# The mask of a windowed attention added by VectorE instead of TensorE, and the row maximum subtracted by GpSimd

## The reference, cut to what matters

```
sim  = einsum('bhwie,bhwje->bhwij', bq, bk2) * QK_SCALE        # 32 x 64 scores a window
mask = (it < jb) | (it > jb + w) | (jb == -1)
sim  = where(mask, -finfo.max, sim)
attn = softmax(sim, -1)
out  = einsum('bhwij,bhwje->bhwie', attn, bv2)
```

## Time and profile before

| | us |
|---|---|
| three timed runs | 5191.45, 5195.39, 5198.09; median 5195.39 |
| the profiled execution: span from its first to its last instruction | 5196.3 |
| its own time | no other figure than its span |
| busy: TensorE, VectorE, ScalarE, GpSimd | 4059.5, 4157.5, 2852.2, 2552.5 |
| one round inside a turn of the loop, and one that begins a turn | 87.4, 91.1 |

### The profile page before, as it was taken

How to read it: one execution, slowest core, us unless ns; L and a number is a source line. 1 busy time by engine, 2 the same in 40 slices (tenths; PEclk the granted TensorE clock), 3 DMA queues, 4 the chain that set the end, 5 groups by cost and what they waited for, 6 DMA issues and landing times. The chain is left out here.

```text
span 5196.3 us, 147973 instructions
## 1 busy us (share of the span) xinstructions
PE 4059.5 (78%) x62298; PEld 2893.8 (56%) x63066; DVE 4157.5 (80%) x6032; ACT 2852.2 (55%) x4736; POOL 2552.5 (49%) x1604
## 2 busy tenths in 40 slices
PE   2012048999979999789999789999799997899996
PEld 2011036666656666566666566666566665666664
DVE  5977978888878888778888788888788887788885
ACT  1011036666656666556666566666566665565665
POOL 3665844544435544445455445445355444454542
PEclk8566579999989999999999999999899999999998
DMA  0000011111111111111111111111111111111112
GB/s 21 0 6 6 0 43 37 25 25 25 25 45 25 25 25 25 33 37 25 25 25 25 33 37 25 25 25 25 46 25 25 25 25 33 37 25 25 25 25 57
DMA packets 86314, 139.19 MB, mean 27 GB/s; under 512 B 14457, under 2 KB 35600, under 8 KB 83984
## 3 DMA queue, kind: packets, MB, share of 16 engines
q1 hardware_dynamic: 78698, 127.06, 9.3%
q10 hardware_dynamic: 6950, 2.39, 0.2%
HBM read 30.59 MB, written 4.46 MB: 7 GB/s over the span
## 5 line engine op out<-in xcount | busy, mean ns | idle before, releaser
L1054 POOL TENSOR_TENSOR kn<-kn,r 128x512 f32<-128x512 f32 x385 | 495.6, 1287 | 1659.0 <-ACT r L968 1659.0
L960 ACT ACTIVATE sq<-ps 128x512 f32<-128x512 f32 x768 | 459.3, 598 | 905.8 <-PE ps L784 901.7
L1090 DVE TENSOR_TENSOR rb<-ps,tab 128x512 f32<-128x512 f32 x768 | 527.7, 687 | 404.7 <-PE ps L784 346.1
L966 ACT ACTIVATE r<-r 128x512 f32<-128x512 f32 x769 | 485.7, 632 | 567.3 <-DVE r L1101 566.7
L1054 POOL TENSOR_TENSOR qn<-qn,r 128x512 f32<-128x512 f32 x384 | 495.4, 1290 | 550.0 <-ACT r L968 550.0
L1047 POOL TENSOR_TENSOR kn<-ra,rb 128x512 f32<-128x512 f32 x384 | 631.2, 1644 | 79.7 <-DVE ra L1092 70.2
L1094 DVE TENSOR_TENSOR sqlo<-sq 128x512 fp32r<-128x512 f32 x768 | 644.9, 840 | 0.0
L782 PE MATMUL ps<-xhs,wl 128*128 128x512 f32 x768 | 403.5, 525 | 237.3 <-PEq L122 178.5
L1101 DVE TENSOR_SCALAR r<-ps 128x512 f32<-128x512 f32 x768 | 524.2, 683 | 29.0 <-remote 10.5
L1047 POOL TENSOR_TENSOR qn<-ra,rb 128x512 f32<-128x512 f32 x384 | 537.6, 1400 | 0.0
L857 PEld LDWEIGHTS ps<-v,pt 64*32 64x32 f32 x24768 | 394.2, 108 | 243.7 <-issue 186.9
(11 more groups left out here) (182 smaller groups left out, 9161.1 us busy)
## 6 DMA issues: line engine op xcount, KB each, us to landing
v<-v SPq DMA_DIRECT2D x96, 768.0 KB, 5.8
v<-v SPq DMA_DIRECT2D x96, 192.0 KB, 5.7
raw<-in_L_ffn_Wqkv SPq DMA_DIRECT2D x7, 1536.0 KB, 7.3
tab<-in_rotary SPq DMA_DIRECT2D x6, 1024.0 KB, 5.7
raw<-in_L_ffn_Wo SPq DMA_DIRECT2D x6, 512.0 KB
sT<-so ACTq DMA_DIRECT2D x3, 768.0 KB, 3.3
xnat<-in_L_attn_hidden_states SPq DMA_DIRECT2D x8, 256.0 KB, 3.4
srow<-sT SPq DMA_DIRECT2D x8, 256.0 KB, 3.1
```

Source lines behind the costliest of these rows:

```text
L960: nc.scalar.activation(sq[:, k, :], ps[:, A, :], ACT.Square).then_inc(cur["sq"], 1)
L966: nc.scalar.activation(r1[:, k, :], r1[:, k, :], ACT.Ln, scale=RN * RN).then_inc(cur["ln"], 1)
L1054: nc.gpsimd.tensor_tensor(dst, dst, r1[:, k, :], ALU.mult).then_inc(cur["qkn"], 1)
L1090: nc.vector.tensor_tensor(rb[:, k, :], ps[:, BB, :], tab[:, 2 * k + 1, :], ALU.mult)
```

## The change

TensorE no longer writes the mask; its scores start their banks anew. VectorE adds the mask, which stays in float32 in the constants' tile, as it moves the scores from PSUM to `pr`, and takes the maximum from `pr`. GpSimd subtracts the maximum in place, at the end of its iteration. There is a new counter "masked": TensorE's scores wait for it, where they waited for "sub", which GpSimd now counts and exp waits for as before. The bf16 copies of the mask and of the identity in the setup are gone, and a block's end waits for GpSimd's last subtraction too.

```diff
             def scores(i):
-                after(pe, "sub", before(i, 1))
-                for e in range(2):
-                    nc.tensor.matmul(ps[:, S0 + e, 0:256], identb[:], maskb[:], start=True, stop=False,
-                                     skip_group_check=True)
+                after(pe, "masked", before(i, 1))
                 pe.wait_ge(cur["qkn"], 2 * i + 1)
...
-                            k[:, wd * WIN:(wd + 2) * WIN], start=False, stop=True, skip_group_check=True,
+                            k[:, wd * WIN:(wd + 2) * WIN], start=True, stop=True, skip_group_check=True,
...
+            def subtract_max(i):                       # GpSimd
+                b = (i - 1) % 2
+                pool.wait_ge(cur["m"], i + 1)
+                p8 = pr[:, b, :].rearrange("p (g k) -> p g k", g=8)
+                nc.gpsimd.tensor_tensor(p8, p8, stat[:, b, 0, :].unsqueeze(2).broadcast_to([P, 8, 64]),
+                                        ALU.subtract).then_inc(cur["sub"], 1)
+
             for i in range(HP):
                 if live(i, 1):
                     normalise(i, 1)
...
                     normalise(i, 0)
+                if live(i, 1):
+                    subtract_max(i)
...
-            def subtract_max(i):
+            def row_max(i):                            # VectorE, called where subtract_max was
                 b = (i - 1) % 2
                 dve.wait_ge(cur["S"], i + 1)
-                s4 = ps[:, S0:S1 + 1, 0:256].rearrange("p e (g k) -> p e g k", g=4)
                 after(dve, "pt", before(i, 2))
-                nc.vector.tensor_reduce(stat[:, b, 0, :].rearrange("p (e g) -> p e g", e=2), s4, AX_X,
+                nc.vector.tensor_tensor(pr[:, b, :].rearrange("p (e k) -> p e k", e=2), ps[:, S0:S1 + 1, 0:256],
+                                        mask.unsqueeze(1).broadcast_to([P, 2, 256]),
+                                        ALU.add).then_inc(cur["masked"], 1)
+                dve.wait_ge(cur["masked"], i + 1)
+                nc.vector.tensor_reduce(stat[:, b, 0, :], pr[:, b, :].rearrange("p (g k) -> p g k", g=8), AX_X,
                                         ALU.max).then_inc(cur["m"], 1)
-                dve.wait_ge(cur["m"], i + 1)
-                nc.vector.tensor_tensor(pr[:, b, :].rearrange("p (e g k) -> p e g k", e=2, g=4), s4,
-                                        stat[:, b, 0, :].rearrange("p (e g) -> p e g", e=2).unsqueeze(3)
-                                        .broadcast_to([P, 2, 4, 64]), ALU.subtract).then_inc(cur["sub"], 1)
```

More of the change, by code:

```diff
@@ L542, in transformer @@
     tab = sb("tab", [P, 4, S])
-    maskb = sb("maskb", [P, 256], BF16)
-    identb = sb("identb", [P, P], BF16)
+    mask = con[:, C_MASK:C_MASK + 256]
     pairr = sb("pairr", [P, P], F32R)
@@ L570, in transformer @@
     s_w = sem("s_w")
-    names = ("xh v vev ab sq sl rot g ssq r ln add qkn S m sub exp rs ri pt ptev o oev ot otev wo x1 "
+    names = ("xh v vev ab sq sl rot g ssq r ln add qkn S masked m sub exp rs ri pt ptev o oev ot otev wo x1 "
              "fx mean fc fq var fe fr fn fh fl w1 gx gl h w2 x2 shifted cleared").split()
@@ L646, in _ @@
             nc.vector.memset(xT[:, B, :], 0.0).then_inc(s_hi, 1)
-            nc.vector.tensor_copy(maskb[:], con[:, C_MASK:C_MASK + 256]).then_inc(s_hi, 1)
-            nc.vector.tensor_copy(identb[:], ident).then_inc(s_hi, 1)
             nc.vector.tensor_copy(pairr[:], con[:, C_PAIR:C_PAIR + P]).then_inc(s_hi, 1)
             nc.vector.tensor_copy(pairb[:], con[:, C_PAIR:C_PAIR + P]).then_inc(s_hi, 1)
-            dve.wait_ge(s_hi, 7)
+            dve.wait_ge(s_hi, 5)
             dve.wait_ge(s_vz, 3)
@@ L759, in round_ @@
         counts = {**dict.fromkeys("rot g ssq add qkn".split(), 2 * HP),
-                  **dict.fromkeys("oev ptev otev sub o S ri ot pt".split(), HP), "xh": 4}
+                  **dict.fromkeys("oev ptev otev sub masked o S ri ot pt".split(), HP), "xh": 4}
         def after(eng, name, n):
@@ L1175, in vector @@
                 if live(i, 1):
-                    subtract_max(i)
+                    row_max(i)
                 if i == 2 and full:
@@ L1202, in _ @@
                 pool.wait_ge(sets[0]["qkn"], 1 if drain else 2 * HP)
+                pool.wait_ge(sets[0]["sub"], 1 if drain else HP)
             @block.vector
@@ L1232, in _ @@
                 pool.wait_ge(sets[0]["qkn"], 2 * HP)
+                pool.wait_ge(sets[0]["sub"], HP)
             @block.sync
```

## The result

The changed kernel takes 5462.4 us (median of 4, 5454.9 to 5466.6) against 5195.1: 1.0509 times the time before, 95% interval 1.0496 to 1.0521. Slower, as forecast, and 3 us from the forecast time.

A forecast was written before the change was run, and what follows sets the result against it. No engine is full; a loop between VectorE and TensorE sets the iteration. 255 us over 48 rounds, 16 at block ends and about 1 of drain make 272 on 5196.3; forecast 5465 us, range 5350 to 5560.

The forecast's parts named there:

- Mask matmuls and VectorE's pair at nothing: Removing TensorE's mask matmuls (119 us) gains zero; VectorE's new add and maximum cost the same as its old pair.
- The order in i=6, 2.84 us: In iteration 6 exp starts 2.84 us late, because GpSimd's subtraction stands behind the put-off normalise(5,0); nothing covers it.
- The subtraction, 1.29 us: GpSimd's new 128x512 subtraction takes 1.29 us per iteration, with 1.10 and 1.55 kept as alternatives.
- my lower bound of 1.10: Cheapest GpSimd subtraction considered, 1.10 us, a sixth of a broadcast product; about 4.5 us a round, 5426 in all.
- 2.10: Time from the old L1111's start until exp can start, via maximum, semaphores and GpSimd's subtraction: 2.10 us.
- i=4 and i=5, 0.67 and 1.15: Iterations 4 and 5 lengthen by exp's full delay, 0.67 and 1.15 us, since consumers stand right behind exp.
- i=0, 1 and 2, 0, 0.06 and 0.60: Iterations 0, 1 and 2 lengthen by 0, 0.06 and 0.60 us, existing waits covering the rest of exp's delay.
- the long wait for guard(0,0): In iteration 0, TensorE's squares(0,1) waits for VectorE's guard(0,0) longer than exp's 0.71 us delay, so cost 0.
- The clock stays up: TensorE's granted clock does not fall in iteration 6's stall; the rival that it falls had chance 0.18, 5550 us.
- my price of 1.8 us a round: Estimated cost if TensorE's clock fell in iteration 6: 1.8 us in each of 48 rounds, 85 us more.
- Ends of blocks, 16 us: At two barriers per layer GpSimd's last subtraction ends 1.35 us later than VectorE's did; times 12, 16 us.
- 5.32 us a round: Lengthening of one round of eight iterations: 0.67 + 1.15 + 2.84 + 0.06 + 0.60; 255 us over 48 rounds.

The follow-up runs named there:

- e3: The kernel before without the mask matmuls, scores left unmasked, all else as it was: 5206.7 us, 1.0014.
- e2: The changed kernel with added matmuls in iteration 6 that only keep TensorE busy while it waits for exp and normalise: 5384.8 us, 1.0359.
- e1: The changed kernel with GpSimd's subtraction in iteration 5 moved ahead of normalise(5,0): 5267.5 us, 1.0132.
- e7: The kernel before with GpSimd's rotations of i = 0, 1, 2 and 5 waiting for VectorE's split of the squares: 5072.1 us, 0.9761.
- e4: The changed kernel with the subtraction on VectorE behind the maximum, in place in SBUF, instead of on GpSimd: 5350.6 us, 1.0295.
- e5: e1 with ScalarE's v copies of iterations 2 and 4 and gates of iteration 5 ahead of exp: 5256.7 us, 1.0103.

## Why the prediction was right, and where its parts were not

- *Mask matmuls and VectorE's pair at nothing*: right, by e3 and by 1366 against 1371 ns.
- *The order in i=6, 2.84 us*: right in mechanism. e2, which has the wait and not the clock, gives 13.94 - 11.27 = 2.67; e1 without it 0.09, and that is not the subtraction's: without the mask matmuls alone (e3) i=6 is 11.37 too.
- *The subtraction, 1.29 us*: too dear. 1.04 us is its median, under my lower bound of 1.10, which came from broadcast products of another shape. Exp could start 1.84 us after the old L1111, not 2.10.
- *i=4 and i=5, 0.67 and 1.15*: 0.41 and 0.94; the difference, 0.26 and 0.21, is the cheaper subtraction.
- *i=0, 1 and 2, 0, 0.06 and 0.60*: measured -0.49, -0.36 and +0.17. Here a step failed: I had seen that a late GpSimd lets the split go ahead in i=1, and let squares(i,1) wait for a late turn_out instead; for i=0 I kept the long wait for guard(0,0). In the changed kernel the split takes 0.86 us in i=0 instead of 1.67, and squares(0,1) to squares(2,1) follow turn_out without a wait for guard. With the cheaper subtraction turn_out is earlier, so a gain remains. How much of it is the split's and how much the subtraction's, no run separates; e7 shows that in the kernel before the split's order alone is worth more, 1.00 in i=0 and 0.70 in i=1.
- *The clock stays up*: failed. It fell in 45 of 48 rounds and cost 78 us (e2); my price of 1.8 us a round was near the 1.7 measured.
- *Ends of blocks, 16 us*: ScalarE's pause before the next layer's weights, at the end of five blocks, was 4.88 to 5.45 us and is 5.99 to 6.43, 1.1 us more in the mean, as 1.35 less the 0.25 of the cheaper subtraction makes it. At the other six ends, behind lone rounds, i=7 takes 18.70 us in e1 and e2 against 17.46, 1.24 more (medians). The twelve come to some 14. (The row at 2178.06 is the end of a block of seven rounds, not of a lone round; the count is the same.)

So 5.32 us a round without the clock was too much by 2.04 (98 us over 48 rounds; e2's round is 3.28 us above that before), and 78 us of clock and some 30 at ends of blocks, turns of the loop and the first rounds of a layer, half of which I had counted, filled the place. The time was hit by luck, because two errors cancelled; the direction and the place were right for the reason given, that exp(6) could not start earlier in the order that the code gives.

## What to carry to other kernels

An idle engine is not a free one: in an in-order program ask what the moved instruction queues behind, at each place of the loop, above all where another step was put off; here that one place made 195 of 267 us, with the clock that fell in its stall. Moved ahead of one instruction, the same subtraction on the same engine beat the version on VectorE (e1 and e4). Look also for gaps that an edit opens on TensorE: in e5 the clock's fall took back most of what the edit had won. When a change makes an engine late and some iterations get shorter, look for what it got out of the way of: that contention was worth 2.4% by one wait, in the unchanged kernel.

## What the runs showed of the hardware

- A GpSimd subtraction with one operand broadcast along rows of 64 took 1.04 us, the same shape with two full operands 1.29. Size didn't tell it, nor did the products of the earlier trace rows. The 1.29 is a product's, and a sum of two full operands took 1.28 where nothing held it; no subtraction of two full operands was run, so that it is the broadcast which makes it cheaper is not shown.
- TensorE's clock fell to its lower level (0.50) after two gaps of 1.41 and 1.80 us with about 1 us of work between them, in 45 of 48 rounds; in e2, with the gaps filled, in none. In e5 it fell in 39 of 48; in the round read, TensorE had waited 1.27 and 0.61 us with one pair of squares matmuls between. No run shows what tells these rounds from the others.
- A VectorE instruction with two SBUF operands and a GpSimd one hold each other for their whole length: whichever starts second ends only a fixed time after the first. In the kernel before, all 212 splits that met a running GpSimd instruction ended 0.55 to 0.58 us after it (0.68 us alone), and all 382 GpSimd instructions that met a running split ended 1.13 to 1.15 us after that (1.28 alone). The Trainium skill (GPSIMD Engine Reference, section 1, Specifications) says that the two engines share SBUF interfaces and that VectorE instructions with two SBUF inputs contend; the split of 1.67 us agrees, and L1110, with one operand in PSUM, stayed at 0.68.
